# A convolution layer ahead of an attention: chunks 1 to 3 normalised in one call, correlations scaled on their way out of PSUM, and two layers' loops interleaved

## The reference

```python
# layer 0, "conv": 25 local correlations of unit vectors, then a 1x1 convolution
norm = sqrt(sum(feature * feature, axis=1)); fn = feature / maximum(norm, 1e-12)
corr = stack([sum(pad(fn)[:, :, r:h+r, cc:w+cc] * fn, axis=1) for cc in range(5) for r in range(5)])
y    = relu(einsum('oc,bchw->bohw', conv_w, concatenate([feature, corr])) + conv_b)
# layer 1, "attention": 32 heads of 8 channels, softmax over the batch axis
qkv  = einsum('brnd,ed->brne', xr, w_qkv) + b_qkv
out  = einsum('brnm,brmd->brnd', softmax(einsum('brnd,brmd->brnm', q, k), axis=0), v)
# layer 2: o = gamma * (x x^T)(W x) + x      layer 3: a mixture of 8 experts, the best 2 of each token
```

## Time and profile before

| | us |
|---|---|
| median of 3 runs | 678.34 (672.76 to 682.39) |
| the profiled execution: its own time | 677.54 |
| its span (first to last instruction) | 675.4 |
| mean granted clock of TensorE | 0.91 of full speed |
| busy: PE, DVE, POOL, ACT | 575.6, 474.9, 383.0, 327.3 |

### The profile page before, as it was taken

One profiled execution on the slowest core, in us unless ns is written; L12 is line 12 of the kernel. 1 busy time (PEld: TensorE's weight loads), 2 busy tenths in 40 slices (PEclk: granted clock), 3 DMA queues, 4 the chain that ended last, 5 costly groups with the idle time before them and its releaser, 6 DMA issues.

```text
span 675.4 us, 13252 instructions
## 1 busy us (share of the span) xinstructions
PE 575.6 (85%) x4548; PEld 363.4 (54%) x4549; DVE 474.9 (70%) x835; ACT 327.3 (48%) x707; POOL 383.0 (57%) x237
## 2 busy tenths in 40 slices
PE   3777786899999999999999998589973899999955
PEld 2444443665555555555555554479862465656533
DVE  3434675689999999999999999384568233333326
ACT  2344377366776676767667766133231233333310
POOL 1000037289999999999999999321002565656520
PEclk9777889589999999999999999599965899999995
DMA  8811105622222112222112200000012222222229
GB/s 276 328 34 33 32 23 203 251 83 96 73 67 64 62 60 71 71 68 65 61 60 69 71 2 1 1 0 1 33 46 52 81 87 80 88 78 87 71 87 333
DMA packets 30500, 56.56 MB, mean 84 GB/s; under 512 B 8342, under 2 KB 22319, under 8 KB 29423
## 3 DMA queue, kind: packets, MB, share of 16 engines
q1 hardware_dynamic: 25694, 38.97, 17.4%
q0 software_dynamic: 3744, 10.39, 5.0%
q10 hardware_dynamic: 1008, 6.49, 2.4%
HBM read 38.43 MB, written 17.40 MB: 83 GB/s over the span
## 4 chain that ended last, share of the span: by engine, by line
POOL 39%; PE 34%; issue 9%; DVE 8%; ACT 4%; DMA 3%; another core or an unknown queue 1%; SPq 1%; POOLq 1%; ACTq 0%
POOL e_ring L353 38%; PE ps L1235 9%; PE ps L1251 5%; PE ps L978 2%; PE ps L1002 2%; PE ps L1167 2%; PE ps L1227 2%; PE ps L1046 2%; DVE stats L628 2%; PE ps L1189 2%; PE ps L991 1%; PE ps L1125 1%; PE ps L1180 1%; ACT x_hat L419 1%
## 5 line engine op out<-in xcount | busy, mean ns | idle before, releaser
L353 POOL TENSOR_TENSOR e_ring<-e_ring,x_hat 128x1024 f32<-128x1024 f32 x128 | 272.7, 2134 | 37.0 <-ACT x_hat L527 25.0
L517 ACT ACTIVATE e_ring<-ps 128x1024 f32<-128x1024 f32 x128 | 131.0, 1024 | 96.0 <-PE ps L1072 96.0
L736 DVE TENSOR_REDUCE m_bf<-ps 128x128 bf16<-128x1024 f32 x128 | 156.3, 1221 | 10.5 <-PE ps L1063 10.4
L743 DVE TENSOR_REDUCE x_hat<-e_ring 128x128 f32<-128x1024 f32 x128 | 155.8, 1217 | 3.1 <-ACT e_ring L517 3.1
L1063 PE MATMUL ps<-q_stack,k_stack 72*128 72x128 bf16 x1024 | 140.1, 321 | 8.8 <-DMA k_stack<-qk_parts 8.8
L1063 PEld LDWEIGHTS ps<-q_stack,k_stack 72*128 72x128 bf16 x1024 | 104.8, 133 | 35.6 <-issue 35.5
L1072 PE MATMUL ps<-m_bf,ident_neg 128*128 128x512 bf16 x256 | 81.0, 399 | 13.4 <-DVE m_bf L736 5.8
L1086 PE MATMUL ps<-e_ring,v_slot 128*32 128x128 f32 x2048 | 86.0, 285 | 3.6 <-POOL e_ring L353 3.6
L1086 PEld LDWEIGHTS ps<-e_ring,v_slot 128*32 128x32 f32 x2048 | 50.0, 109 | 58.0 <-issue 53.0
L1235 PE MATMUL ps<-w_sb,e_ring 128*128 x156 | 75.3, 606 | 0.8 <-issue 0.7
L386 POOL DMA_INDIRECT pair_rows<-scratch,slot_y x39 | 38.4, 986 | 43.7 <-DVE scratch L940 28.7
(11 more groups left out here) (149 smaller groups left out, 700.9 us busy)
## 6 DMA issues: line engine op xcount, KB each, us to landing
q_stack<-qk_parts SPq DMA_DIRECT2D x32, 288.0 KB
k_stack<-qk_parts SPq DMA_DIRECT2D x96, 96.0 KB
w_sb<-in_w13T_dram ACTq DMA_DIRECT2D x2, 2048.0 KB, 9.8
qk_parts<-e_ring SPq DMA_DIRECT2D x2, 1536.0 KB, 6.5
qk_parts<-scratch SPq DMA_DIRECT2D x2, 1536.0 KB, 18.5
x_res<-in_x_dram SPq DMA_DIRECT2D x8, 256.0 KB, 3.9
w_sb<-in_w2T_dram ACTq DMA_DIRECT2D x2, 1024.0 KB, 15.3
token_rows<-work SPq DMA_DIRECT2D x4, 512.0 KB, 3.0
```

The costliest lines, as they stand in the source:

```text
L353: nc.gpsimd.tensor_tensor(ev, ev, view(x_hat, CH + (u % RS) * P, [[0, BQ], [1, P], [0, 2]]), ALU.mult).then_inc(norm_done, 1)
L517: nc.scalar.activation(e_ring[:, u % ER, :], score_banks(v), ACT.Exp).then_inc(exp_done, 1)
L736: nc.vector.tensor_reduce(m_bf[:, u % 2], by_position(score_banks(v).rearrange("p a c -> p (a c)")), AXY, ALU.max).then_inc(max_done, 1)
L743: nc.vector.tensor_reduce(s_sum[:, u % 2], by_position(e_ring[:, u % ER, :]), AXY, ALU.add).then_inc(sum_done, 1)
```

## The change

1. Group norm of layer 0: chunk 0 alone, chunks 1 to 3 in one call each of `group_norm`, `variance`, `deviation` and `second_half` (n = 3, 24 columns in place of 8, 12 values in place of 4).
2. `unit_vectors` is gone. `gram` multiplies `x_hat` itself; DVE scales each row of a gram tile by the neighbour's 1/norm as it leaves PSUM, and the turned correlations by the position's own 1/norm; both copies were ACT's. `rnorm` has a buffer for each chunk. The squares' sums go to bank 5 (`NORM_BANK`) instead of bank 0, shared with `group_norm`.
3. New order: the trip of chunk t-1 is picked up in turn t after `norms(t)`; in PE's turn, norms, features, gram, transposes, features, correlations follow each other. Layer 1's group norms and the first four q/k tiles are woven into the end of layer 0.
4. The q/k tiles run half by half, chunk by chunk, q and k in turn (`QK_TILES`); the first 8 use two banks. q and k of half 0 are stored as chunks 0 to 2 (1152 KB each) and then chunk 3 (384 KB each).
5. The experts' weights are loaded as 24 transfers of 256 KB by SP, one behind each `load_stack` of groups 2 to 7; SP's loop over groups is written out.

```diff
-        rnorm = scratch[:, 0:CH]
-        GST = CH
+        rnorm = [scratch[:, i * CH:(i + 1) * CH] for i in range(NCH)]
+        GST = NCH * CH
...
+        QK_TILES = [(s, c) for half in range(H) for c in range(NCH) for s in (2 * half, 2 * half + 1)]
+        QK_BANK = [2 + n % 2 if n < 2 * NCH else n % 4 for n in range(2 * H * NCH)]
+        NORM_BANK = 5
...
+            weights = ([(w13_sb[:, h, n * 2 * C:(n + 1) * 2 * C], w13T[h, :, n * 2 * C:(n + 1) * 2 * C]) for n in range(E) for h in range(H)]
+                       + [(w2_sb[:, f, n * 2 * C:(n + 1) * 2 * C], w2T[f, :, n * 2 * C:(n + 1) * 2 * C]) for n in range(E // 2) for f in range(2)])
...
+                store_parts(0, s, 0, T - CH, 2 * NCH - 3 + s)
+            for s in range(2):
+                store_parts(0, s, T - CH, T, 2 * NCH - 1 + s)
             for n in range(2):
-                sp.wait_ge(parts_out[n], 16)
+                sp.wait_ge(parts_out[n], 32)
             for i in range(HPG):
                 load_stack(0, i)
...
-            with sp.Fori(1, NG - 1) as g:
+            for g in range(1, NG - 1):
                 for i in range(HPG):
                     sp.wait_ge(scores_done, g * UPG + 4 * (i + 1))
                     load_stack(g + 1, i)
+                    sp.dma_start(*weights[(g - 1) * HPG + i]).then_inc(w_in, 16)
...
-            act.wait_ge(x_in[NCH - 1], 16 * H)
-            for dst, src in ((w13_sb[:, 0, :], w13T[0]), (w13_sb[:, 1, :], w13T[1]), (w2_sb[:, 0, :], w2T[0]), (w2_sb[:, 1, :], w2T[1])):
-                act.dma_start(dst, src).then_inc(w_in, 16)
...
+            inverse_norms(0)
+            deviation(0, 1, NCH - 1)
+            for c in (1, 2):
+                normalise(0, c)
+                squares_of(c)
+            inverse_norms(1)
+            normalise(0, 3)
+            squares_of(3)
+            conv_out(0)
+            inverse_norms(2)
+            conv_out(1)
+            inverse_norms(3)
+            deviation(1, 0)
+            normalise(1, 0)
+            conv_out(2)
             act.wait_ge(consts_in, 16 * LATER)
+            deviation(1, 1)
+            qk_tile(0)
+            normalise(1, 1)
+            qk_tile(1)
+            conv_out(3)
+            deviation(1, 2)
+            normalise(1, 2)
+            qk_tile(2)
+            qk_tile(3)
+            deviation(1, 3)
+            normalise(1, 3)
+            for n in range(4, 2 * H * NCH):
+                qk_tile(n)
+            second_part(2 * H * NCH - 1)
...
-            def unit_vectors(c):
...
+            def gram_rows(c):
+
                 dve.wait_ge(rn_done, c + 1)
-                nc.vector.tensor_tensor(view(work, c * CH, [[T, H], [1, CH]]), x_hat[:, :, nc_cols],
-                                        view(scratch, 0, [[0, H], [1, CH]]), ALU.mult).then_inc(fn_done, 1)
-                dve.wait_ge(fn_done, c + 1)
+                if c == 0:
+                    dve.wait_ge(pool_init, 1)
+                if c >= 2:
+                    dve.wait_ge(gram_out[c - 2], 16)
+                for t in range(TPC):
+                    i, hb = c * TPC + t, t % 2
+                    dve.wait_ge(gram_done, i + 1)
+                    off = GST + (c % 2) * TPC * ROW + t * ROW + (0 if hb else REACH)
+                    q0 = (t // 2) * N + (P - REACH if hb else 0)
+                    nc.vector.tensor_tensor(view(scratch, off, [[1, ROW - REACH]]), ps[:, 2 + i % 2, 0:ROW - REACH],
+                                            rnorm[c][:, q0:q0 + ROW - REACH], ALU.mult).then_inc(gram_row, 1)
+
+            def turned_correlations(d):
+
+                dve.wait_ge(cor_tr, d + 1)
+                nc.vector.tensor_tensor(cor_t[:, d * CH:(d + 1) * CH], ps[0:NK, 0, :], rnorm[d][0:NK], ALU.mult
+                                        ).then_inc(cor_t_done, 1)
...
+            dve.wait_ge(x_in[0], 16 * H)
+            statistics(0, 0)
+            variance(0, 0)
+            second_half(0, 0)
+            for c in range(1, NCH):
+                dve.wait_ge(x_in[c], 16 * H)
+                statistics(0, c)
+            floor_of_norms(0)
+            variance(0, 1, NCH - 1)
+            gram_rows(0)
+            second_half(0, 1, NCH - 1)
+            for t in range(1, NCH):
+                floor_of_norms(t)
+                correlations(t - 1)
+                if t >= 2:
+                    add_conv(t - 2)
+                if t >= 3:
+                    variance(1, t - 3)
+                gram_rows(t)
+                if t >= 3:
+                    second_half(1, t - 3)
+                turned_correlations(t - 1)
+                if t >= 2:
+                    statistics(1, t - 2)
+            dve.wait_ge(consts_in, 16 * LATER)
+            add_conv(2)
+            correlations(3)
+            variance(1, 1)
+            turned_correlations(3)
+            second_half(1, 1)
+            statistics(1, 2)
+            qk_tile(0)
+            qk_tile(1)
+            variance(1, 2)
+            add_conv(3)
+            second_half(1, 2)
+            statistics(1, 3)
+            qk_tile(2)
+            qk_tile(3)
+            variance(1, 3)
+            second_half(1, 3)
+            for n in range(4, 2 * H * NCH):
+                qk_tile(n)
...
+                if k < 2 and (k, c) != (0, 0):
+                    pe.wait_ge(n2_floor, 1 if k == 0 else NCH)
...
+                normed(0, BPC * (c + 1) - 1)
...
+                if n == 0:
+                    pe.wait_ge(consts_in, 16 * LATER)
+                    pe.wait_ge(gram_row, TILES)
+                    pe.wait_ge(relu_done, H * (NCH - 1))
                 normed(1, BPC * (c + 1) - 1)
-                if n >= 4:
-                    pe.wait_ge(rest_done, n - 3)
-                nc.tensor.matmul(bank(n % 4), qkv_sb[:, s % 2], x_hat[:, h, c * CH:(c + 1) * CH],
+                if n == 2 * NCH:
+                    pe.wait_ge(relu_done, H * NCH)
+                if n >= 2:
+                    pe.wait_ge(rest_done, n - 1 if n < 2 * NCH else n - 3)
...
+            group_norm(0, 0)
+            conv_features(0, 0)
+            norms(0)
+            group_norm(0, 1, NCH - 1)
+            gram(0)
+            conv_features(0, 1)
+            for t in range(1, NCH):
+                norms(t)
+                conv_features(t, 0)
+                if t >= 3:
+                    group_norm(1, t - 3)
+                gram(t)
+                turn_correlations(t - 1)
+                conv_features(t, 1)
+                conv_correlations(t - 1)
+            group_norm(1, 1)
+            qk_tile(0)
+            turn_correlations(3)
+            qk_tile(1)
+            conv_correlations(3)
+            group_norm(1, 2)
+            qk_tile(2)
+            qk_tile(3)
+            group_norm(1, 3)
+            for n in range(4, 2 * H * NCH):
+                qk_tile(n)
...
+            pe.wait_ge(w_in, 16 * (NG - 2) * HPG)
```

More of the change, by code:

```diff
@@ L343, in _ @@
             pool.wait_ge(pool_init, 2)
-            for n in range(2 * H * NCH):
-                s, c = n // NCH, n % NCH
+            for n, (s, c) in enumerate(QK_TILES):
                 pool.wait_ge(part2, n + 1)
@@ L430, in squares_of, with inverse_norms @@
                                      ACT.Square).then_inc(sq_done, 1)
[L432 to L446 removed]
+            def inverse_norms(c):
+                act.wait_ge(n2_floor, c + 1)
+                power(rnorm[c], rnorm[c], rn_done)
             def conv_out(d):
@@ new lines, in second_half @@
+            def second_half(k, c, n=1):
+                dve.wait_ge(gn_rstd, gn_calls(k, c))
+                mean, var, rstd = (gn[:, c:c + n, i] for i in range(3))
+                tmp = gn_tmp[:, 0:n]
+                link(nc.vector.scalar_tensor_tensor(out=tmp, in0=rstd, scalar=-0.5, in1=rstd, op0=ALU.mult, op1=ALU.mult))
+                link(nc.vector.tensor_tensor(tmp, tmp, var, ALU.mult))
+                link(nc.vector.scalar_tensor_tensor(out=rstd, in0=tmp, scalar=1.5, in1=rstd, op0=ALU.add, op1=ALU.mult))
+                nc.vector.scalar_tensor_tensor(out=gn[:, c:c + n, 3], in0=mean, scalar=-1.0, in1=rstd, op0=ALU.mult,
+                                               op1=ALU.mult).then_inc(gn_coef, 1)
+                dve.wait_ge(gn_coef, gn_calls(k, c))
+                for j in range(c, c + n):
+                    for i in range(BPC):
+                        cols = slice((j * BPC + i) * N, (j * BPC + i + 1) * N)
+                        nc.vector.tensor_scalar(x_hat[:, 1, cols], x_res[:, 1, cols], gn[:, j, 2, BPC + i:BPC + i + 1],
+                                                gn[:, j, 3, BPC + i:BPC + i + 1], ALU.mult, ALU.add).then_inc(xhat_dve, 1)
@@ L683, in add_conv, with qk_tile @@
                 dve.wait_ge(x1_done, d + 1)
[L685 to L716 removed]
+            def qk_tile(n):
+                s, c = QK_TILES[n]
                 dve.wait_ge(part1, n + 1)
+                if n == 3:
+                    dve.wait_ge(y_done, H * NCH)
                 if n >= 4:
                     dve.wait_ge(part3, n - 3)
```

(11 more changed lines are left out.)

197 lines of the change are left out of this document (50 added, 147 removed).

## The result

The changed kernel takes 659.92 us (median of 4 runs, 658.73 to 662.43); the kernel before, in 4 runs on the same chip, 677.2. The ratio is 0.975, 95% interval 0.9701 to 0.9799: faster. The profiled execution took 658.73 us, its span is 656.4.

What follows compares the result with a forecast made beforehand. The prediction took the attention's start as what matters, set by layer 0, the q/k tiles up to the eighth, the store and the load. Starting it 20.5 us earlier gave 677.5 - 20.5 = 657 us, range 652 to 664.

Steps and rivals of the forecast that it cites:

- (a): Layer 0's start: chunk 0's features and norms at half speed, 3.7 us each, so norms(1) at 25.7 us.
- (b): Layer 0's three turns at full speed: 10.0 us each instead of 18.2, conv_correlations(2) ending 30.6 later at 56.3.
- the slack of 0.7: In layer 0's turns, 0.7 us to spare before DVE's wait for the previous chunk's store and load, called the tightest place.
- (c): End of layer 0 through layer 1's group norms, four tiles woven in: DVE nearly the bound, 19.4 us, to 76.3.
- half speed in the weaving: Rival: PE at half speed in the weaving and first tiles only, costing 5 to 12 us: 662 to 669, chance 13%.
- (d): Tiles 4 to 15: ACT paces them at 1.31 us each; last ends at 92.6, tile 7's third part at 83.9.
- (e): Storing half 0's q and k, 3072 KB: the pieces queue, so it ends at 89.8 us, or 86.9 if they don't.
- (f): Head 0's load before the attention: 10.0 us unchanged, to 99.8; with half of (c)'s 1 us, 100.3.
- (g): Weights as 24 transfers of 256 KB during the attention: cost nothing, against 64 us without that cover.
- What follows keeps its length: From the attention's start on: everything keeps its length, so the 20.5 us gained at the start carry to the end.
- the attention starts better: Rival: a shorter gap keeps full speed, 4 us less, or the store's pieces don't queue, 3 less: 649 to 654, chance 12%.

Runs made afterwards that it cites:

- e12: The changed kernel again, unchanged, profiled a second time on the same chip as e11: 655.99 us, ratio 0.968.
- e1: The changed kernel with the experts' weights loaded at the start again, four transfers in ScalarE's queue: 659.75 us, ratio 0.983.
- e2: The changed kernel with q and k of half 0 stored in two whole pieces of 1536 KB: 659.78 us, ratio 0.980.
- e3: The changed kernel with q and k of half 0 stored in six pieces, the first two issued early: 655.45 us, ratio 0.975.
- e9: e3 plus SyncE waiting for head 0's load before issuing those of heads 1 to 3: 657.2 us, ratio 0.972.
- e7: The kernel before the change with only the weights' load moved, as 24 transfers in the attention: 678.23 us, ratio 1.003.
- after: The changed kernel as first measured and profiled: 659.92 us, ratio 0.975.
- e10: The changed kernel with 14 unused PE matmuls of 128x256 in the gap before the attention: 659.64 us, ratio 0.977.
- e6: The changed kernel with both the six-piece store of e3 and POOL's later start of e5: 658.23 us, ratio 0.974.
- e4: The changed kernel without weaving, all 16 q/k tiles following layer 1's last group norm: 660.91 us, ratio 0.980.
- e5: The changed kernel with POOL's third parts waiting for the last variance of layer 1: 661.39 us, ratio 0.976.
- e8: The kernel before the change with four unused PE matmuls ahead of conv_correlations in turns 0 to 2: 670.38 us, ratio 0.990.
- e11: The changed kernel with the edits of e3, e9 and e10 together (10 matmuls): 655.3 us, ratio 0.967.

## Why the prediction was right, step by step

The forecast was 657 (range 652 to 664); the first group gave 659.92, the second (e12) 655.99. The mechanism was the predicted one: PE's list without ACT's thread in it, full speed in the turns, the store's backlog, the load. The steps, predicted and measured in the profile after:

- (a) *The start* was mis-sized: `norms(1)` 25.7, measured 23.77. I took features and `norms` of chunk 0 at half speed, 3.7 each; only the features were (3.39 for four), `norms` took 1.88.
- (b) *Three turns* 30.6, measured 31.25 (23.77 to 55.02): 10.1, 10.1 and 11.0. The scaled row took 0.33 (taken 0.35), gram 2.57 (2.33), and no wait for the band, so the slack of 0.7 was enough. That it hung on the weights' move, e1 shows.
- (c) *Weaving* was the step that I underestimated most: 20.0 from the end of `conv_correlations(2)`, measured 21.98 (55.02 to 77.0). 1.7 us are the three stretched instructions (0.40, 0.98 and 0.32 over 0.17), which no row of before shows, since POOL began there after the group norms. DVE also waited 1.66 us for PE, whose half-speed tile stood ahead of the transposes. That is the rival *half speed in the weaving*: the granted clock was 0.69 there, as it says; but its price was under 2 us, not 5 to 12, since DVE set the pace and the tiles from 76 us on ran at 1.00. The Trainium skill's rule ("TensorE: Matmul & The Clock Gate", "HAM oscillation") puts such half speed down to idle gaps between groups of matmuls. This trace agrees for one of three drops, that at 72.2, behind 3.03 us of idle PE; at 55.2 and 65.5 the clock fell while PE was busy, with no gap over 0.3 us in the 10 us before.
- (d) *Tiles*: from there to the eighth third part 7.6, measured 8.05; last tile on DVE 92.6, measured 93.5.
- (e) *The store* 5.9 after that third part, measured 6.25; e2 and e3 give 8.56 and 4.17 for the coarser and the finer split, so the queued pieces were the right reading.
- (f) *The load* 10.0, and 0.5 for the clock: 10.5, measured 8.73. Here the agreement is partly luck: (a) and (f) were too long by 1.93 and 1.77 us, (b), (c), (d) and (e) too short by 0.65, 1.98, 0.45 and 0.35, and together that makes 100.04 against 100.3. The load isn't a constant: 8.7 to 10.5 from issue to scores in the profiles with all heads behind it, 10.1 in e12, and 8.8 with head 0's alone (e9).
- (g) *The weights in the attention* cost 0, predicted and measured (e1, e7, after). The Trainium skill's advice in "DMA: Bandwidth & Descriptors", "Rules for kernel authors", of 1 MiB or more per transfer isn't contradicted as to bandwidth: each 256 KB needed 6.7 us to land. It just doesn't matter under that cover of 12 units.
- *What follows keeps its length*: true of the attention and the router's stage in these two profiles. For the attention that is luck too, since it goes by how long the half speed lasts, and both had 20 us of it. The loop's 1.6 us and the runs' spread are the difference to the result.
- The rival *the attention starts better* failed: the gap was shorter (7.88 instead of 8.85) and the clock still fell to 0.50. e10 shows that its premise was right and its price too (5.0; I had 4): it needs PE busy, not a somewhat shorter gap (e6's was 5.38 us, and its half speed lasted 31.1).

What stays open: why the router's stage takes 95.8 or 99.1, and the loop 126 to 132. In the stage, the clock is at 0.50 for 11.6 to 12.0 us from the attention's end in the seven profiles with the short stage, and for 13.2 to 14.5 in the seven with the long one; so the two go together, but what decides it wasn't tried. The same is open for the attention's opening: the half speed lasted 7 to 31 us behind gaps of 5 to 11 us, and not longer behind the longer gaps. In the loop, the long ones hold pieces of "issue" in front of ACT (16.2 us at L612 in after, none in e1) that the profile doesn't name. It took 126.4 to 127.5 us in e1 to e4, which ran on one chip, and 127.8 to 132.2 in e5 to e8, e11 and e12, on one other chip, so it varies on one chip as well. Of the change's parts, the group norm of three chunks in one call and the order of the q/k tiles were not tried alone.

## What to carry to other kernels

An engine's idle time is paid twice where it drops TensorE's clock: filling a gap with useless matmuls gave 3 to 4 us a turn here and 5 us at the attention's start, so measure a reorder against that cheap filler before crediting the order. Before taking work off the critical path's queue, ask which small transfer shared it: moving 6 MB was worth nothing alone and 6 to 7 us at the load's issue once the new order needed the trip in time. And where stages behind the change vary by more than its effect, compare milestones in the traces, take a second profile of the unchanged kernel as the measure of what a difference means, and look for what the varying stage follows: here the attention's length followed the time at half speed.

## What the runs showed of the hardware

**DVE's smallest instructions can wait for POOL's whole one.** Those with all inputs in SBUF and two of them (L644, L653, and L663 to L665 of e5) ended with the POOL instruction beside them, up to 0.98 us late, and the profile of e12 has the same three durations (0.57, 1.15, 0.49); L720 and L724, which read one input from PSUM, kept 0.74 and 0.41 beside POOL. The Trainium skill states this ("SBUF — State Buffer", "SBUF: two separate sides"): DVE and GpSimd share one pair of ports as an exclusive lock, held for the whole instruction, and a DVE instruction with two SBUF inputs needs it. The traces agree: in the profile after, each of the three ends 0.02 us behind POOL's.

**A load's time isn't a constant**: from issue to scores, head 0's 576 KB took 8.73 and 10.09 us in two executions of the same kernel and 10.47 after the finer store, all with three more heads' loads issued behind it, and 8.81 without them.

**A small store beside a 6 MB load** took 10.4 us until the next transfer could go, against 2.9 without.

**The clock's return** isn't the same each time: after the restart at 11.33 PE was at half speed for one group of 3.4 us; after the gap before the attention the granted clock stayed at 0.50 for 20 us though PE was busy for 19.96 of them, and for 7.1 to 31.3 us in the other profiles with that gap; and in e10, without the gap, it never fell there. Each us of it cost the attention some 0.3 us, by the table's line.
